# Cross-attention with layer norm: y of every tile stays in its PSUM bank, and two steps move by one place around batch 5

## The reference

```python
q = emb @ Wq + bq                                # 16 x 100 x 512
k = latent @ Wk + bk ; v = latent @ Wv + bv      # 16 x 722 x 512
w = softmax(q @ k^T / sqrt(512), axis=1)         # over the 100 tokens
x = w @ v + emb
out = (x - mean(x)) * rsqrt(var(x) + 1e-6) * gamma + beta
```

## Time and profile before

| | us |
|---|---|
| median of 3 runs | 143.87 (143.75 to 144.30) |
| the profiled execution | 144.33 |
| its span (first to last recorded event) | 142.6 |
| PE busy | 135.5 (95%) |
| DVE busy | 114.1 (80%) |
| ACT busy | 78.7 (55%) |
| POOL busy | 65.2 (46%) |

### The profile page before, as it was taken

How to read it: one execution, slowest core, us unless ns; L and a number is a source line. 1 busy time by engine, 2 the same in 40 slices (tenths; PEclk the granted TensorE clock), 3 DMA queues, 4 the chain that set the end, 5 groups by cost and what they waited for, 6 DMA issues and landing times.

```text
span 142.6 us, 2971 instructions
## 1 busy us (share of the span) xinstructions
PE 135.5 (95%) x1046; PEld 130.9 (92%) x1046; DVE 114.1 (80%) x221; ACT 78.7 (55%) x282; POOL 65.2 (46%) x61
## 2 busy tenths in 40 slices
PE   6999999999999999989999999999999999999940
PEld 6899999999998999989999999999999999999930
DVE  0379995996997779689999987877789976797993
ACT  4167088577276924574655638474847546386320
POOL 1000000027304681734667553639486645639991
PEclk9999999999999999999999999999999999999996
DMA  4999999936077595986996979697997985635314
GB/s 148 333 397 419 423 300 381 353 156 214 11 260 255 172 390 159 353 342 163 340 319 241 334 259 375 225 336 229 303 305 247 341 291 219 219 114 183 138 43 178
DMA packets 10814, 37.33 MB, mean 262 GB/s; under 512 B 1200, under 2 KB 1456, under 8 KB 10800
## 3 DMA queue, kind: packets, MB, share of 16 engines
q1 hardware_dynamic: 9424, 34.79, 69.8%
q10 hardware_dynamic: 1376, 2.36, 4.4%
HBM read 33.87 MB, written 3.28 MB: 260 GB/s over the span
## 4 chain that ended last, share of the span: by engine, by line
PE 88%; POOL 6%; issue 2%; ACT 1%; DVE 0%; POOLq 0%; DVEq 0%
PE ps_S L419 29%; PE ps_U L433 26%; PE ps_Y L454 10%; PE ps_U L392 6%; PE ps_Y L392 6%; PE ps_Y L337 3%; POOL xT_in L970 2%; POOL xT_in L958 2%; PE ps_S L341 1%; POOL prob L947 1%; PE ps_w L442 1%; PE ps_U L341 1%; PE ps_c L407 1%; POOL rstd L963 1%; PE ps_c L408 1%
## 5 line engine op out<-in xcount | busy, mean ns | idle before, releaser
L578 ACT ACTIVATE expo<-scores,negmax 121x100 f32<-121x100 f32 x96 | 35.0, 366 | 28.4 <-DVE negmax L748 28.4
L419 PE MATMUL ps_S<-G,ctxT_in 128*121 128x100 f32 (+1 forms) x384 | 43.4, 269 | 0.0
L419 PEld LDWEIGHTS ps_S<-G,ctxT_in 128*121 128x121 f32 (+1 forms) x384 | 42.1, 185 | 0.0
L433 PEld LDWEIGHTS ps_U<-prob,ctx_in 121*128 121x128 f32 x336 | 39.4, 192 | 0.9
L433 PE MATMUL ps_U<-prob,ctx_in 121*128 121x100 f32 x336 | 39.6, 274 | 0.0
L947 POOL TENSOR_TENSOR prob<-expo,rinv 121x600 f32<-121x600 f32 x16 | 19.6, 1228 | 31.3 <-DVE rinv L755 31.2
L958 POOL TENSOR_TENSOR xT_in<-x_in,xT_in 128x512 f32<-128x512 f32 (+1 forms) x13 | 16.6, 1281 | 16.7 <-issue 8.6
L759 DVE TENSOR_REDUCE probsum<-prob 121x100 f32<-121x600 f32 x16 | 19.8, 1237 | 4.1 <-POOL prob L947 3.8
L963 POOL TENSOR_TENSOR rstd<-vareps,neg_half 128x1 f32<-128x1 f32 (+1 forms) x13 | 11.7, 902 | 22.9 <-DVE vareps L786 22.9
L744 DVE TENSOR_TENSOR scores<-ps_S,c_rows 121x600 f32<-121x600 f32 x16 | 12.5, 779 | 9.7 <-PE ps_S L419 6.7
L578 ACT ACTIVATION_READ_ACCUMULATOR expo<-scores,negmax 121x1 f32 x96 | 18.0, 187 | 0.0
(11 more groups left out here) (122 smaller groups left out, 184.4 us busy)
## 6 DMA issues: line engine op xcount, KB each, us to landing
ctx_in<-ctx SPq DMA_DIRECT2D x16, 768.0 KB, 5.1
ctxT_in<-ctxT SPq DMA_DIRECT2D x16, 722.0 KB, 4.3
xT_in<-xT SPq DMA_DIRECT2D x8, 400.0 KB, 9.1
x_in<-x SPq DMA_DIRECT2D x12, 256.0 KB, 4.4
out<-xT_in ACTq DMA_DIRECT2D x8, 256.0 KB, 4.2
wqk<-Wqk SPq DMA_DIRECT2D x4, 388.0 KB, 4.9
out<-xT_in SPq DMA_DIRECT2D x3, 256.0 KB, 2.0
wv_in<-Wv SPq DMA_DIRECT2D x1, 512.0 KB, 15.3
```

The lines of the kernel that those rows point to most:

```text
L419: last = nc.tensor.matmul(ps_scores(c)[0:rows(c), :], ctxT_in[:, q, l * M + c * MP:l * M + c * MP + rows(c)], G[:, l, bass.ds(b * T, T)], ...
L433: last = nc.tensor.matmul(ps_U[:, q, l * T:(l + 1) * T], ctx_in[0:rows(c), q, c, l * P:(l + 1) * P], prob[0:rows(c), q, c * T:(c + 1) * T] ...
L578: last = nc.scalar.activation(expo[0:MP, q, c * T:(c + 1) * T], scores[0:MP, q, c * T:(c + 1) * T], ACT.Exp, bias=negmax[0:MP, q, c:c + 1] ...
```

## The change

1. y is no longer a tile of its own. `add_residual` writes Y + residual back into the bank of `ps_Y` from which it reads, and `row_stats`, `centred_rows` and `centred_half` read `ps_Y`. PE therefore waits, before it writes a bank of `ps_Y` again, until the tile two before is centred (`centred_set`) instead of until its y is added (`y_set`): in `values`, and at the two places at the end.
2. On ACT, `take_shift(2)` stands between turn 4 and turn 5 instead of between turn 5 and turn 6.
3. On DVE, the first two of the four terms of `weigh_by_u` for group 3 stand ahead of `chunk_sum(4)` inside turn 5 instead of behind it. (Turn 5 is written out for this; the other steps in it are those that `turn(5, 1)` runs, since no tile ends with batch 2.)

```diff
-        y = wv_in
...
                 if j >= 2:
-                    pe.wait_ge(y_set, j - 1)
+                    pe.wait_ge(centred_set, j - 1)
...
-            pe.wait_ge(y_set, NT - 3)
+            pe.wait_ge(centred_set, NT - 3)
...
-            pe.wait_ge(y_set, NT - 2)
+            pe.wait_ge(centred_set, NT - 2)
...
             turn(4, 0)
-            turn(5, 1)
             take_shift(2)
-            each_turn(turn, 6, 9)
+            each_turn(turn, 5, 9)
...
-                nc.vector.tensor_tensor(y[0:n, q, :], ps_Y[0:n, q, :], resid[0:n, q, :], ALU.add).then_inc(y_set, 1)
+                nc.vector.tensor_tensor(ps_Y[0:n, q, :], ps_Y[0:n, q, :], resid[0:n, q, :], ALU.add).then_inc(y_set, 1)
...
-                nc.vector.bn_stats(stats[0:n, q, :], y[0:n, q, :]).then_inc(stats_set, 1)
+                nc.vector.bn_stats(stats[0:n, q, :], ps_Y[0:n, q, :]).then_inc(stats_set, 1)
...
-                nc.vector.scalar_tensor_tensor(centred[0:n, q, :], y[0:n, q, :], meanvar[0:n, q, 0:1], gamma_rows[0:n, :],
+                nc.vector.scalar_tensor_tensor(centred[0:n, q, :], ps_Y[0:n, q, :], meanvar[0:n, q, 0:1], gamma_rows[0:n, :],
                                                ALU.subtract, ALU.mult).then_inc(centred_set, 1)
...
             centre(1)
-            turn(5, 1)
+            lower_U(2, 0)
+            normaliser(4, 0)
+            maxima(5, 1)
             weigh_by_u(3, (0, 1))
+            chunk_sum(4, 0)
             turn(6, 0)
...
-                nc.vector.scalar_tensor_tensor(centred[:, q, halves[h]], y[:, q, halves[h]], meanvar[:, q, 0:1],
+                nc.vector.scalar_tensor_tensor(centred[:, q, halves[h]], ps_Y[:, q, halves[h]], meanvar[:, q, 0:1],
                                                gamma_rows[:, halves[h]], ALU.subtract, ALU.mult).then_inc(done, 1)
```

## The result

The changed kernel takes 142.62 us (median of 14 runs, 142.18 to 143.42) against 143.88 (14 runs, 142.96 to 144.47). The ratio is 0.9924, with a 95% interval of 0.9904 to 0.9945, so it is 0.8% faster; by the interval, between 0.8 and 1.4 us. The forecast was 142.8, with a range from 142.5 to 143.8. (One execution in the experiments, the profiled one of e1, took 772 us: PE's score matmuls were 966 ns long in the mean instead of some 270, at a granted clock of 1.0, while the instructions of the other engines had their usual length. Why isn't known; that kernel was profiled again as e5, and only e5's trace is used.)

What follows compares the result with a forecast made beforehand. PE was taken to bound the kernel (88% of the span), with POOL at the very end (6%). Gains of 0.62 (turn 6), 0.15 (turn 7) and 0.3 (tail) sum to 1.07 us: 143.87 - 1.07 = 142.8, range 142.5 to 143.8.

Steps and rivals of the forecast that it cites:

- PE's waits: PE stands 0.62 us in turn 6 and 0.15 in turn 7 before `values`; the rest of the middle is closed.
- The DVE edit and its disturbance: DVE, turn 5: moved terms use 1.46 us of idle time, L724 stands beside POOL's prob; PE's 0.62 us goes.
- The case with y in SBUF: Turn 5 with prob(4) where it was: U_lo ends at 62.95, PE starts at 63.05 instead of 63.62.
- rstd at 0.55 and prob 0.4 earlier: POOL: rstd takes 0.55 us for all tiles, 0.45 less; in turn 5 `finish(1)` comes up to 0.43 earlier, then prob(4).
- Turn 7, the race: Turn 6: rinv of batch 5 at 62.91, POOL's residual at 62.96; the order gives +0.15 or -0.22 us.
- Rival B: POOL's residual starts first in turn 6; PE waits 0.37 us in turn 7, not 0.15; 143.17 us, chance 0.22.
- y in PSUM costs next to nothing on DVE: Statistics and centring on DVE from PSUM: 0.01 us per tile, taken as 0.
- Rival C: PSUM dearer on DVE: 0.2 us late in turns 6, 7 and tail; gain about 0.6, 143.3 us; chance 0.08.
- The new PE wait on the centring: `values(j)` waits for centring of tile j - 2; nearest at L534, margin 1.54 us, 1.8 without hold-up; cost 0.
- Rival E: PE waits at L534 or L517 for the centring; 2.5 us late means slower, 144.6 us and more; chance 0.07.
- The ACT edit at nothing: ACT's copy L571, moved from ahead of U_hi of batch 3: worth 0 to 0.1 us, taken as 0; cost 0.
- The tail: At the kernel's end, earlier rstd, scaling and finishes bring 0.3 us (ends 0 and 0.45).

Runs made afterwards that it cites:

- e1: The changed kernel with its DVE edit and ACT edit undone, so only y in PSUM stays; ratio 0.9916 to the kernel before.
- e5: The same kernel as e1 (only y in PSUM), run and profiled again; ratio 0.9920 to the kernel before.
- e2: The kernel before with the DVE edit alone, y in SBUF; ratio 0.9934 to the kernel before.
- e3: The kernel before with the DVE edit and the ACT edit, y in SBUF; ratio 0.9971 to the kernel before.
- e7: The changed kernel with an unused DVE memset ahead of rinv of batch 5 in turn 6; ratio 1.0063 to the kernel before.
- e4: The changed kernel with only its ACT edit undone; ratio 0.9914 to the kernel before.
- e6: The changed kernel run again, nothing altered; ratio 0.9915 to the kernel before.
- e8: The kernel before, y in SBUF, with the centring taking gamma from PSUM from turn 13 on; ratio 0.9998 to the kernel before.

## Why the prediction was right, and where it wasn't

- **PE's waits are the only place in the middle:** right. 0.62 and 0.15 were read, 0.63 and 0.16 went.
- **The DVE edit and its disturbance:** right in mechanism. L724 (now L722) is 1.31 us long, as a blocked one, and in the changed kernel the two terms, `chunk_sum(4)` and U_lo end within 0.1 us of what was worked out. The case with y in SBUF has two slips that cancel. L724 was put "in the middle of prob(4)", but its start of 59.50 lies ahead of prob at 59.71; in e2 it goes first, and L728 is the one that stands. And 60.90 + 0.2 + 0.6 + 1.15 is 62.85, not 62.6, by which PE would have kept 0.3 us of its wait. e2 has U_lo's start at 61.52, which is 62.53 on the trace of before, and PE doesn't wait. The 0.05 came out near that by luck.
- **rstd at 0.55 and prob 0.4 earlier:** right (0.56, and prob at 58.91 against 59.71, of which 0.39 is the earlier start of the whole trace).
- **What each part is worth:** here the prediction told too little. It took the DVE edit as the main cause (0.57 of the 0.62, or 0.54 as the lower end) and y in PSUM as what rounds it off. e5 shows that y in PSUM alone leaves 0.18 of the 0.62. Either of the two is nearly enough for turn 6; the sum was unaffected by that.
- **Turn 7, the race:** the forecast's case held, with the lead that was worked out (0.05 us; 0.03 measured). Rival B's mechanism is shown in e3 and e7. Its price was right for y in SBUF (0.37 worked out, 0.38 measured) and wrong for the changed kernel, to which the prediction applied it. The step that failed is the one that followed DVE after the lost race with the distances of the trace of before: those have a POOL that is late by its long rstd. With the short one L728 (L727 in e7) loses the next race, and 0.37 became 2.5 us in e7's trace. As far as e7, with its memset, stands for B, that rival was no "143.17" but slower than before.
- **y in PSUM costs next to nothing on DVE:** right. Statistics 698 ns against 693, centring 743 against 742 in the last tile before, adding in place 691 against 681 to SBUF: some 15 ns a tile. Rival C held back that the two rows of the last tile ran when PE was at its end; these are the means of ten and eleven tiles made while PE was at work, so C falls. The surcharge of the Trainium skill (Perfetto Trace Analysis) that was weighed there, 60 ns against 125 ns, does not show in these rows.
- **The new PE wait on the centring:** right; PE starts L533 at 134.10, tile 10 is centred at 132.28, so the margin is 1.8 us, as worked out. (Rival E's own sum was loose: 2.5 us late would only use up the gain, and its 144.6 needs 3.3.)
- **The ACT edit at nothing:** right for the changed kernel (e4), but it was taken as harmless, and it isn't: it costs 0.37 us with y in SBUF (e3) and the margin of the race otherwise.
- **The tail:** 0.3 given, 0.31 measured, by the steps named: 0.17 of the 0.23 us for which L896 waited, and 0.14 on DVE, where 0.1 was given.
- **The sum:** 1.07 given, 1.06 in the trace, 1.09 by the ratio. That it came this close has some luck in it: it stands on a race that was put at nearly even. The range's lower end of 142.5 isn't the case that was named for it: with the tail at 0.45 the sum gives 142.65, and the measured median is 142.62. By the prediction's own bar, below 143.15, that is "faster", to which it gave 0.53.

## What to carry to other kernels

Where VectorE and GpSimd work side by side on SBUF, read every instruction that is longer in one row than in its neighbours: it shows who stood for whom, and moving one of the two tensors that the centring reads to PSUM ended that here at some 15 ns a tile. A step that is moved into a gap can stand there for what runs beside it (L722 took 1.31 us for 0.47), so count it at that length before you call the gap wide enough. And an edit that brings another engine forward (here ACT's copy) can cost without touching the critical engine, by changing who starts first. After a change that frees an engine, work out its next instructions again from the new times and not from the old trace, since what it is free to do is what it can collide with.

## What the runs showed of the hardware that I had not expected

A DVE instruction of six columns that starts 0.06 us after a POOL instruction of 512 columns stood for all of it (1.25 us for 0.17), and one that started 0.03 us before it lost nothing (0.02 in e6). The recorded starts don't decide so near a race: L727 in e7 is recorded 0.02 us ahead of POOL's too and still stood for 1.1 us. Its recorded start, 68.30, lies inside the centring in front of it on DVE (67.64 to 68.38), so it may have begun to read only after POOL's 68.32; no run separates this. The Trainium skill (SBUF — State Buffer, Who interferes with whom) says that a DVE instruction with two SBUF inputs contends with a GpSimd instruction that reads SBUF, that the lock is exclusive, and that the order of issue decides who blocks. These runs agree, and e8 shows that one of the two tensors in PSUM is enough to end it. L724, with one tensor in SBUF and two scalars per partition, stood as well (1.31 for 0.47). Not every such meeting is gone from the changed kernel, nor does each cost time: rinv stands for 0.75 us in turns 7 and 8 (at 69.02 and 75.85), as before, and PE waits in neither. And a single race lost at one place of a DVE queue cost 2.5 us in e7's trace, over six times what the same loss cost with y in SBUF, because each turn's timing decided the next turn's race.
